# A causal convolution as full 128x128 matmuls, or as four 64x64 quarters of the array a tap

## The chip, the cores and the metric

The kernel runs on one core of a Trainium2 chip. Times are device microseconds of that core; the profile's times are microseconds from the start of its span unless they are marked ns. TensorE does the matmuls (PE in the profile, its weight loads PEld), VectorE (DVE) elementwise work and the scans, ScalarE (ACT) activations and most of the copies out of PSUM, GpSimd (POOL) further elementwise work and the indirect DMAs, SyncE (SP) issues the other DMAs.

## The reference, cut to what matters

```
xz = x @ in_proj_w.T + in_proj_b              # x: 4 batches x 2048 positions x 256
x_in, z = jnp.split(xz, 2, axis=-1)           # 512 channels each
x_pad = jnp.pad(x_in, ((0, 0), (3, 0), (0, 0)))
x_conv = sum(x_pad[:, k:k + L, :] * conv_w[None, None, :, k] for k in range(4)) + conv_b
x_conv = silu(x_conv)
x_dbl = x_conv @ x_proj_w.T                   # dt_low (64), B (16), C (16)
dt = softplus(dt_low @ dt_proj_w.T + dt_proj_b)
# scan over positions, 16 states for each of the 512 channels:
#   h = exp(dt * A) * h + (exp(dt * A) - 1) / A * B * x_conv
#   y = sum over the states of h * C, + D * x_conv
x = layernorm(x + (y * silu(z)) @ out_proj_w.T + out_proj_b)
# then 16 experts, the best 2 of each row, a shared expert and a second layernorm
```

Everything is float32. The change touches the line with the four taps.

## The kernel before

The first part of the program (`mamba`) works in 16 units of 512 positions. The 512 channels are four chunks of 128, one channel a partition. A unit has 64 items (4 chunks x 16 states): VectorE scans an item along the 512 positions, GpSimd or VectorE multiplies the result by C, and TensorE adds it into `y_ps` with a matmul by a diagonal (L1040). For the states of kind "f" TensorE also makes the scan's input with four small matmuls (L1062, `make_du`), for which VectorE's line L1226 waits.

The order of work is written out by hand. A unit is a loop over 64 slots, and in slot m each engine does item m and then whatever the tables place there. The table `PLACE` gives the slot in which each further tile of TensorE begins: `x0` to `x3` are the input projection, `c0` to `c3` the convolution, `low`, `bc`, `d0` to `d3` lead to dt, `T0` to `T3` are transposes, `r0` to `r3` the skip term, `z0` to `z3` the gate, `o0`, `o1` the output projection, `t0`, `t1`, `lg`, `pf` belong to the routing. A tile has one to four parts, and one part is done a slot. The tiles go in turn into two PSUM banks (`work`), so a tile can begin only when the tile two before it has been copied out; the semaphores are `filled` and `emptied`. The tiles of kind x, c, low, T, d for the next unit are made during this one.

A chunk's convolution is four matmuls of 128 rows by 128 columns by 512 positions, one for each tap (L1115): the weights are a diagonal matrix of the tap's factors (`dg_tap`), the moving data is `x_in`, shifted by one position a tap, with three columns of the previous unit in front. ScalarE copies the sum out with the bias (L856), in the slot after the tile's last part, and applies silu to two chunks at once in slots 10 and 38 (L957).

Every engine runs its instructions in the order in which they stand. An instruction that waits holds up all behind it on its engine.

Of the kernel before, what the change touches and what calls it, by code (L numbers as in the profile page):

```python
# [28 lines left out]
P = 128  # L29
T = 512  # L30
# [3 lines left out]
DI = 512  # L34
CH = DI // P
KT = DM // P
NS = 16
TAPS = 4
HALO = TAPS - 1
RANK = 64  # L40
TT = T // P
EPS = 1e-5
NE = 16
IF = 128
# [75 lines left out]
class Kept:  # L120

    def __init__(self, nc):
# [13 lines left out]
        self.full = sb("full", [P, P], BF16)  # L136
        self.rows = sb("x_tok", [P, TT, ROW])
        self.x_tok = self.rows[:, :, 0:DM]
        self.home_steps = sb("home_steps", [P, 2, TT])
        self.y_gated = sb("y_gated", [P, CH, T])  # L140
        self.room = sb("room", [P, (NE + 1) * DM])
        self.stats = sb("stats", [P, TT, 6])
        self.mean_var = sb("mean_var", [P, TT, 2])
        self.spread = sb("spread", [P, TT])
        self.shift = self.stats[:, :, 0]
# [24 lines left out]
def mamba(nc, d):  # L170
# [5 lines left out]
    with ExitStack() as ctx:  # L176
# [10 lines left out]
        w_in = sb("w_in", [P, KT, 2 * DI])  # L187
# [3 lines left out]
        b_in = sb("b_in", [P, 2 * CH])  # L191
        taps = sb("taps", [P, CH, TAPS])
# [9 lines left out]
        dg_tap = kept.room[:, 0:CH * TAPS * P].rearrange("p (c k t) -> p c k t", c=CH, k=TAPS)  # L202
# [19 lines left out]
        x_in = kept.room[:, CH * TAPS * P:CH * (TAPS * P + HALO + T)].rearrange("p (c t) -> p c t", c=CH)  # L222
# [24 lines left out]
        work = psum("work", [P, 2, T])  # L247
# [28 lines left out]
        filled = [sem(f"work_filled{q}") for q in range(2)]  # L276
# [62 lines left out]
        def pool_slot(s):  # L339
# [11 lines left out]
        NEXT = ["x0", "x1", "x2", "x3", "c0", "c1", "c2", "c3", "low", "bc", "d0", "d1", "T0", "T1", "z0", "z1"]  # L351
        OWN = ["d2", "d3", "T2", "T3", "r0", "r1", "r2", "r3", "z2", "z3"]
        ROUTING = ["o0", "o1", "t0", "t1", "lg", "pf"]
        PLACE = [("x1", 0), ("x0", 1), ("c0", 3), ("c1", 5), ("d3", 8), ("T2", 9), ("T3", 10), ("d2", 12), ("o0", 16), ("o1",
# [3 lines left out]
        U_AT = [-2, -1, None, 1, None, 6, 7, None, 8, None, 15, 18, 19, None, 25, None, 28, 31, None, 32, None, 37, 39, None, 41,  # L358
# [62 lines left out]
        def emptied_all(eng, plan, unit, tiles):  # L421

            most = {}
            for t in sorted(tiles, key=ORDER.get):
                most[plan.bank(t)] = t
            for bank, t in most.items():
                eng.wait_ge(emptied[bank], plan.before(t, unit) + 1)
# [588 lines left out]
        def _(pe):  # L1016
# [48 lines left out]
            def tile(u, plan, t, part):  # L1065

                n, q, nq = later(u), u[1] % 2, (u[1] + 1) % 2
                bank = plan.bank(t)
                if part == 0:
                    wait(pe, emptied[bank], plan.before(t, u))  # L1070
                out = work[:, bank]
                if t in ("t0", "t1"):
                    k = int(t[1])
                    pe.wait_ge(normed, count(u, TT, 0))
                    for tt in range(TT):
                        mm = nc.tensor.transpose(work[:, bank, tt * P:(tt + 1) * P], x_tok[:, tt, k * P:(k + 1) * P], ident[:])
                elif t == "lg":
                    logits = work[:, bank, 0:TT * NE].rearrange("p (t e) -> p t e", e=NE)
                    if part == 0:
                        emptied_all(pe, plan, u, ["t0", "t1"])  # L1080
                        nc.tensor.matmul(logits, ones[:], b_gate[:].unsqueeze(1).to_broadcast([1, TT, NE]), start=True, stop=False)
                    for k in range(KT):
                        mm = nc.tensor.matmul(logits[:, part], x1_t[:, k, part * P:(part + 1) * P], w_gate[:, k],
                                              start=False, stop=(part == TT - 1 and k == KT - 1))
                elif t == "pf":
                    pe.wait_ge(route, count(later(u, -1), ROUTE, 5))
                    mm = number_places(work[:, bank, 0:(TT + 1) * NE])
                elif t == "low":
                    c = part
                    if c % 2 == 0:  # L1090
                        pe.wait_ge(x_conv_ready, count(n, 2, c // 2 + 1))
                    mm = nc.tensor.matmul(work[0:RANK + 2 * NS, bank], w_x[:, c], x_conv[:, nq, c], start=(c == 0), stop=(c == CH - 1))
                elif t == "bc":
                    emptied_all(pe, plan, u, ["low"])
                    for k in range(TT):
                        mm = nc.tensor.matmul(work[:, bank, k * 2 * NS:(k + 1) * 2 * NS], bc_rows[:, k * P:(k + 1) * P],
                                              ident[RANK:RANK + 2 * NS, RANK:RANK + 2 * NS], start=True, stop=True)
                elif t[0] == "x":
                    if t in ("x0", "x1") and part == 0:
                        pe.wait_ge(x_t_in[nq], loads(n))  # L1100
                    m, k = int(t[1]), part
                    mm = nc.tensor.matmul(out, w_in[:, k, m * P:(m + 1) * P], x_t[:, nq, k], start=(k == 0), stop=(k == KT - 1))  # L1102
                elif t[0] == "z":
                    m, k = int(t[1]) + CH, part
                    src = q if t in ("z2", "z3") else nq
                    mm = nc.tensor.matmul(out, w_in[:, k, m * P:(m + 1) * P], x_t[:, src, k], start=(k == 0), stop=(k == KT - 1))  # L1106
                elif t[0] == "c":
                    c, k = int(t[1]), part
                    if plan is first and c < 2 and k == 0:
                        pe.wait_ge(diags_ready, 1)  # L1110
                        pe.wait_ge(later_in, 16 * (len(LATER) + 2))
                    if k == 0:
                        pe.wait_ge(halo_moved, count(n, 2, 1))
                        emptied_all(pe, plan, u, [f"x{c}"])
                    mm = nc.tensor.matmul(out, dg_tap[:, c, k], x_in[:, c, k:k + T], start=(k == 0), stop=(k == TAPS - 1))  # L1115
                elif t[0] == "T":
                    c = int(t[1])
                    own, src = (u, q) if c >= 2 else (n, nq)
                    pe.wait_ge(x_conv_ready, count(own, 2, c // 2 + 1))
                    for k in range(TT):  # L1120
                        mm = nc.tensor.transpose(work[:, bank, k * P:(k + 1) * P], x_conv[:, src, c, k * P:(k + 1) * P], ident[:])
                elif t[0] == "d":
                    c = int(t[1])
                    if c < 2:
                        emptied_all(pe, plan, u, ["low"])
                    mm = nc.tensor.matmul(out, w_dt[:, c * P:(c + 1) * P], dt_low, start=True, stop=True)
                elif t[0] == "r":
                    c = int(t[1])
                    if c == 0:
                        pe.wait_ge(both_ready, count(u, 1, 1))  # L1130
                    mm = nc.tensor.matmul(out, skip_rows[:, c * P:(c + 1) * P], both[:], start=True, stop=True)
                elif t[0] == "o":
                    if part == 0:
                        pe.wait_ge(gated, count(u, CH, 0))

                    tt, rest_of_it = divmod(part, 2)
                    tok = (2 * int(t[1]) + tt) * P
                    o = work[:, bank, tt * DM:(tt + 1) * DM]
                    if not rest_of_it:
                        nc.tensor.matmul(o, kept.full[0:2 * 32 + 1], b_out_parts[:], start=True, stop=False)  # L1140
                    for c in (range(1, CH) if rest_of_it else (0,)):
                        mm = nc.tensor.matmul(o, y_gated[:, c, tok:tok + P], w_out[:, c], start=False, stop=(c == CH - 1))
                if part == parts_of(t) - 1:
                    mm.then_inc(filled[bank], 1)
# [290 lines left out]
def moe_layout(g, chunks):  # L1435

    import numpy as np

    def stack(name):
        return np.concatenate([g[f"L0_ffn_experts_{name}"], g[f"L0_ffn_shared_{name}"][None]])  # L1440

    up = np.concatenate([stack("wg"), stack("wu")], axis=2)
    return {
        "w_gate": chunks(g["L0_ffn_gate_w"]),
        "b_gate": g["L0_ffn_gate_b"][None],
        "d_row": g["L0_attn_D"][None],
        "w_up": up.reshape(NE + 1, KT, P, 2 * IF).transpose(2, 0, 1, 3),
        "w_down": stack("wd").transpose(1, 0, 2),
    }
# [834 lines left out]
```

## Time and profile before

| what | value |
|---|---|
| time, median of 3 runs | 2742.09 us (2737.33 to 2742.41) |
| span of the profiled execution, first to last instruction | 2716.5 us |
| PE busy | 2518.4 us, 93% of the span |
| DVE busy | 2283.9 us, 84% |
| POOL busy | 2286.1 us, 84% |
| ACT busy | 1832.6 us, 67% |
| mean granted clock of TensorE | 0.975 |

The profile shows the profiled execution's span only; what lies around it is the difference to a run's time, 25.6 us with the median. PE's busy time includes the overlap of consecutive matmuls, so it says that there was always one in flight, not that the array was at its peak. One float32 matmul appears as two MATMUL records and two LDWEIGHTS records: 256 convolution matmuls are x512 in the profile.

### The profile page before, as it was taken

The page shows a single profiled execution, that of the slowest core. Times are in us where ns is not written, and L with a number is a line of the kernel's source. Part 1 is how long each engine was busy: PE and PEld are TensorE (multiplying, and loading weights), DVE is VectorE, ACT ScalarE, POOL GpSimd, SP SyncE. Part 2 cuts the span into 40 slices and gives each one's busy share as a digit, 9 for nine tenths or more (in the row PEclk, how much of TensorE's full clock was granted, in tenths as well). Part 3 has the DMA queues.
Part 4 walks back from the last instruction along what each step waited for, and adds up shares of the span by engine and source line. Part 5 has one row for each costly group of instructions (what it writes and reads, how often), then busy time and mean ns, then how long its engine had stood idle before and what let it go on. Part 6 is the DMA issues. An engine that isn't in the chain of part 4 may idle for free. (4 is left out here: it accounts for less than half of the span.)

```text
span 2716.5 us, 37230 instructions
## 1 busy us (share of the span) xinstructions
PE 2518.4 (93%) x9666; PEld 1447.6 (53%) x9666; DVE 2283.9 (84%) x3740; ACT 1832.6 (67%) x3655; POOL 2286.1 (84%) x2127
## 2 busy tenths in 40 slices
PE   6899999999999999999999999999999988799997
PEld 3445555555545455545555555455554544488874
DVE  3898989898989898889898998989898989755546
ACT  5576767777686767676868676777767675355537
POOL 2899898989898989899898989898989898666654
PEclk8999999999999999999999999999999989899999
DMA  3233343434333434343334334343333334478667
GB/s 89 96 112 113 107 129 103 130 101 125 111 118 108 119 106 121 113 120 115 113 119 116 111 111 127 105 130 101 125 110 117 112 106 138 156 218 249 206 202 245
DMA packets 249004, 349.65 MB, mean 129 GB/s; under 512 B 75863, under 2 KB 123611, under 8 KB 248412
## 3 DMA queue, kind: packets, MB, share of 16 engines
q1 hardware_dynamic: 233196, 302.47, 37.3%
q0 software_dynamic: 15600, 44.79, 4.7%
q8 instruction: 83, 1.36, 0.2%
q14 instruction: 125, 1.02, 0.1%
HBM read 288.72 MB, written 58.45 MB: 128 GB/s over the span
## 5 line engine op out<-in xcount | busy, mean ns | idle before, releaser
L685 POOL TENSOR_TENSOR hc<-h,c_rep 128x512 f32<-128x512 f32 x832 | 1048.2, 1271 | 99.8 <-DMA c_rep<-bc_rows 47.4
L1040 PE MATMUL y_ps<-hc,dg_inv 128*128 128x512 f32 x1664 | 857.6, 607 | 17.6 <-POOL hc L685 15.4
L668 POOL TENSOR_TENSOR h<-x_conv,b_rep 128x512 f32<-128x512 f32 x640 | 803.9, 1269 | 35.3 <-PE y_ps L1040 14.1
L1233 DVE TENSOR_TENSOR_SCAN h<-a_ps,carry,h 128x512 f32<-128x512 f32 x640 | 807.6, 1270 | 9.7 <-ACT score L836 5.4
L778 ACT ACTIVATE a_ps<-dt,a_mat 128x512 f32<-128x512 f32 x640 | 438.6, 687 | 411.4 <-DVE h L1233 408.0
L1062 PEld LDWEIGHTS g_ps<-b_steps,x_conv_rows 128*128 128x128 f32 x3072 | 404.2, 194 | 232.4 <-issue 200.4
L1217 DVE SCALAR_TENSOR_TENSOR h<-a_ps,h 128x512 f32<-128x512 f32 x640 | 428.3, 669 | 92.4 <-ACT a_ps L778 92.3
L1040 PEld LDWEIGHTS y_ps<-hc,dg_inv 128*128 128x128 f32 x1664 | 286.8, 191 | 305.2 <-issue 226.5
L1062 PE MATMUL g_ps<-b_steps,x_conv_rows 128*128 128x128 f32 x3072 | 413.5, 278 | 30.4 <-ACT x_conv_rows L861 16.9
L778 ACT ACTIVATE h<-dt,a_mat 128x512 f32<-128x512 f32 x384 | 268.9, 712 | 60.8 <-POOL hc L685 60.5
L1241 DVE TENSOR_TENSOR_SCAN h<-g_ps,carry,h 128x512 f32<-128x512 f32 x192 | 245.4, 1278 | 24.0 <-ACT h L778 20.6
L1115 PE MATMUL work<-room 128*128 128x512 f32 x512 | 248.8, 595 | 7.8 <-ACT room L849 7.8
L1040 PE MATMUL y_ps<-hc,ident 128*128 128x512 f32 x384 | 217.4, 651 | 38.7 <-DVE hc L1251 38.7
L1241 DVE TENSOR_TENSOR_SCAN g_ps<-g_ps,carry,h 128x512 f32<-128x512 f32 x192 | 246.9, 1286 | 6.3 <-DVE skip L1269 0.5
L1758 POOL DMA_INDIRECT y_planes<-gathered,home x144 | 138.6, 962 | 98.4 <-DVE gathered L2162 74.9
L1102 PE MATMUL work<-x_t,w_in 128*128 128x512 f32 x256 | 140.3, 645 | 63.1 <-DVE x_tok L1284 36.8
L1933 PE MATMUL banks<-w_up,gathered 128*128 x576 | 149.7, 383 | 0.0
L1106 PE MATMUL work<-x_t,w_in 128*128 128x512 f32 x256 | 142.3, 651 | 4.1 <-ACT dt L878 2.1
L1115 PEld LDWEIGHTS work<-room 128*128 128x128 f32 x512 | 91.6, 191 | 95.4 <-issue 94.2
L1251 DVE SCALAR_TENSOR_TENSOR hc<-g_ps,a_inv,c_rep 128x512 f32<-128x512 f32 x192 | 142.0, 739 | 0.0
L650 POOL DMA_INDIRECT slot_rows<-x_tok,place x120 | 121.6, 1013 | 23.2 <-issue 12.2
L1040 PEld LDWEIGHTS y_ps<-hc,ident 128*128 128x128 f32 x384 | 70.6, 200 | 117.8 <-issue 70.7
(269 smaller groups left out, 3479.6 us busy)
## 6 DMA issues: line engine op xcount, KB each, us to landing
c_rep<-bc_rows SPq DMA_DIRECT2D x512, 256.0 KB, 3.4
b_rep<-bc_rows SPq DMA_DIRECT2D x320, 256.0 KB, 3.7
gathered<-slot_rows SPq DMA_DIRECT2D x144, 129.5 KB, 3.5
gathered<-y_planes SPq DMA_DIRECT2D x32, 512.0 KB, 7.7
x_t<-in_x_t SPq DMA_DIRECT2D x16, 512.0 KB, 4.5
x_tok<-in_x_tok SPq DMA_DIRECT2D x16, 512.0 KB, 4.1
out<-x_t SPq DMA_DIRECT2D x16, 512.0 KB, 3.1
x_t_rows<-y_gated SPq DMA_DIRECT2D x15, 512.0 KB, 2.6
```

The lines of the kernel that those rows point to most:

```text
L668: nc.gpsimd.tensor_tensor(h[:, i % SLOTS, e], x_conv[:, u[1] % 2, chunk(i, e)], b_rep[:, n % BS], ALU.mult).then_inc(u_ready, 1)
L685: nc.gpsimd.tensor_tensor(hc[:, i % HCS, e], h[:, i % SLOTS, e], c_rep[:, i % CS], ALU.mult).then_inc(hc_pool, 1)
L778: nc.scalar.activation(out, dt[:, c], ACT.Exp, scale=a_mat[:, c, s:s + 1]).then_inc(made, 1)
L1040: nc.tensor.matmul(y_ps[:, e], by, hc[:, i % HCS, e], start=first_one, stop=(i % HALF == HALF - 1)).then_inc(summed, 1)
L1062: one = nc.tensor.matmul(g_ps[:, e, k * P:(k + 1) * P], x_rows[:, c, k], b_steps[:, f, k], start=True, stop=True)
L1106: mm = nc.tensor.matmul(out, w_in[:, k, m * P:(m + 1) * P], x_t[:, src, k], start=(k == 0), stop=(k == KT - 1))
L1115: mm = nc.tensor.matmul(out, dg_tap[:, c, k], x_in[:, c, k:k + T], start=(k == 0), stop=(k == TAPS - 1))
L1217: nc.vector.scalar_tensor_tensor(out=slot, in0=a_ps[:, e], scalar=1.0, in1=slot, op0=ALU.subtract, op1=ALU.mult).then_inc(b_ready, 1)
L1233: nc.vector.tensor_tensor_scan(slot, a_ps[:, e], slot, before_it, ALU.mult, ALU.add).then_inc(scanned, 1)
L1241: nc.vector.tensor_tensor_scan(out, g_ps[:, e], slot, before_it, ALU.add, ALU.mult).then_inc(scanned, 1)
L1251: nc.vector.scalar_tensor_tensor(out=hc[:, i % HCS, e], in0=g_ps[:, e], scalar=a_inv[:, c, s:s + 1], in1=c_rep[:, i % CS], op0=ALU.mult, o ...
L1933: one = nc.tensor.matmul(gu_ps[:, k % 2, 0:2 * IF], xt[:, k % 4, h * P:(h + 1) * P], w_up[:, e, h], start=(h == 0), stop=(h == KT - 1))
```

## The change

The two chunks of a pair (c0 with c1, c2 with c3) are convolved together. A diagonal 128x128 matrix has only zeros off its two diagonal 64x64 blocks; the change issues only such blocks. For each tap there are four matmuls of 64 rows by 64 columns by 512 positions, each in another quarter of the array. In the notation (input rows, output partitions) they are, as issued: chunk c rows 0-63 to 0-63; chunk c rows 64-127 to 64-127; chunk c+1 rows 0-63 to 64-127; chunk c+1 rows 64-127 to 0-63. The results of rows 0-63 go to the first tile's bank and those of rows 64-127 to the second's, so the channels of the input projection, its bias and the taps are laid out in another order on the host (`by_quarters`), and what comes out stands in the old order.

The tiles `c0` and `c2` keep their places in the sequence of banks, but do nothing themselves. Their work is done with `c1` and `c3`, a tap a slot, in slots 5 to 8 and 32 to 35. Before, `c0` ran in slots 3 to 6 and `c2` in 31 to 34.

```diff
-        PLACE = [("x1", 0), ("x0", 1), ("c0", 3), ("c1", 5), ("d3", 8), ...
-                 17), ("x2", 22), ("r0", 26), ("x3", 26), ("r1", 27), ("c2", 31), ("c3", 32), ("t1", 35), ...
+        PLACE = [("x1", 0), ("x0", 1), ("c0", 5), ("c1", 5), ("d3", 8), ...
+                 17), ("x2", 22), ("r0", 26), ("x3", 26), ("r1", 27), ("c2", 32), ("c3", 32), ("t1", 35), ...
...
-                elif t[0] == "c":
-                    c, k = int(t[1]), part
+                elif t in ("c0", "c2"):
+                    return
+                elif t in ("c1", "c3"):
+                    c, k = int(t[1]) - 1, part
...
                     if k == 0:
                         pe.wait_ge(halo_moved, count(n, 2, 1))
-                        emptied_all(pe, plan, u, [f"x{c}"])
-                    mm = nc.tensor.matmul(out, dg_tap[:, c, k], x_in[:, c, k:k + T], start=(k == 0), stop=(k == TAPS - 1))
+                        emptied_all(pe, plan, u, [f"x{c}", f"x{c + 1}"])
+                    banks = [work[:, plan.bank(f"c{c + e}")] for e in range(2)]
+                    for e in range(2):
+                        for half, rows in enumerate((slice(0, QUARTER), slice(QUARTER, P))):
+                            at = QUARTER * (e ^ half)
+                            mm = nc.tensor.matmul(banks[half][at:at + QUARTER], dg_tap[rows, c + e, k, rows], x_in[rows, c + e, k:k + T],
+                                                  start=(k == 0), stop=(k == TAPS - 1))
+                            if k == TAPS - 1 and e == 1 and half == 0:
+                                mm.then_inc(filled[plan.bank(f"c{c}")], 1)
...
+    def by_quarters(v):
+        v = v.reshape((CH // 2, 4, QUARTER) + v.shape[1:])
+        return v[:, [0, 3, 1, 2]].reshape((DI,) + v.shape[3:])
```

TensorE's program from slot 3 to slot 8 of a unit, before. The convolution is `work<-room`, in the four rows of one matmul and the two of two:

```order
L1115 MATMUL work<-room 128x512 [waits work_emptied1,halo_moved,work_emptied0]
L1040 MATMUL y_ps<-hc,dg_inv 128x512 [waits hc_pool,gated]
L1115 MATMUL work<-room 128x512
L1040 MATMUL y_ps<-hc,dg_inv 128x512 [waits hc_pool,gated]
L1062 MATMUL g_ps<-b_steps,x_conv_rows 128x128 [waits scanned,work_emptied1,b_steps_ready]
L1062 MATMUL g_ps<-b_steps,x_conv_rows 128x128 x3
L1115 MATMUL work<-room 128x512
L1115 MATMUL work<-room 128x512 [waits work_emptied0,halo_moved,work_emptied1]
L1040 MATMUL y_ps<-hc,dg_inv 128x512 [waits hc_pool]
```

The same place after the change, from the two `y_ps` matmuls of slots 4 and 5 to the tile d3 (`work<-low,dt_out`), which stands behind the last group:

```order
L1041 MATMUL y_ps<-hc,dg_inv 128x512 [waits hc_pool,gated] x2
L1063 MATMUL g_ps<-b_steps,x_conv_rows 128x128 [waits scanned,work_emptied1,b_steps_ready]
L1063 MATMUL g_ps<-b_steps,x_conv_rows 128x128 x3
L1122 MATMUL work<-room 64x512 [waits work_emptied0,halo_moved,work_emptied1]
L1122 MATMUL work<-room 64x512 x3
L1041 MATMUL y_ps<-hc,dg_inv 128x512 [waits hc_pool]
L1063 MATMUL g_ps<-b_steps,x_conv_rows 128x128 [waits scanned,work_emptied1,b_steps_ready]
L1063 MATMUL g_ps<-b_steps,x_conv_rows 128x128 x3
L1122 MATMUL work<-room 64x512 x4
L1041 MATMUL y_ps<-hc,dg_inv 128x512 [waits hc_pool]
L1122 MATMUL work<-room 64x512 x4
```

The two matmuls of slots 3 and 4 are gone, and in each of slots 5 to 8 a group of four stands between matmuls of the full array.

ScalarE's program in slots 7 to 9, before. `x_conv<-work` (L856) is the copy of c0, then of c1; `x_arg<-work` is the first copy of d3:

```order
L778 ACTIVATE a_ps<-dt,a_mat 128x512 [waits scanned]
L856 ACTIVATE x_conv<-work,b_conv 128x512 [waits skip_ready,u_ready,work_filled0]
L792 ACTIVATE carry<-h 128x2 [waits scanned]
L778 ACTIVATE a_ps<-dt,a_mat 128x512 [waits scanned]
L856 ACTIVATE x_conv<-work,b_conv 128x512 [waits work_filled1]
L877 ACTIVATE x_arg<-work,b_dt 128x512 [waits decay_ready,softplus_step,factor_ready,work_filled0]
```

And after:

```order
L779 ACTIVATE a_ps<-dt,a_mat 128x512 [waits scanned]
L793 ACTIVATE carry<-h 128x2 [waits scanned]
L779 ACTIVATE a_ps<-dt,a_mat 128x512 [waits scanned]
L857 ACTIVATE x_conv<-work,b_conv 128x512 [waits skip_ready,u_ready,work_filled0]
L857 ACTIVATE x_conv<-work,b_conv 128x512 [waits work_filled1]
L878 ACTIVATE x_arg<-work,b_dt 128x512 [waits decay_ready,softplus_step,factor_ready,work_filled0]
```

The copy of c0 moved behind one more `a_ps` activation, which waits for a scan.

## Rows read from the trace of the kernel before

**Rows 1.** The page: busy time of each engine.

```profile
PE 2518.4 (93%) x9666; PEld 1447.6 (53%) x9666; DVE 2283.9 (84%) x3740; ACT 1832.6 (67%) x3655; POOL 2286.1 (84%) x2127
```

**Rows 2.** Stretches of one unit: window, length, busy us of each engine (instructions), clock, DMA, GB/s.

```profile
1064.00:1091.00 27.00, 26.43 (x98) 13.87 (x97) 26.52 (x36) 15.62 (x29) 25.83 (x27) 1.00 0.31 89
1091.00:1114.00 23.00, 20.49 (x82) 12.54 (x80) 18.11 (x24) 16.11 (x25) 22.44 (x19) 0.99 0.61 176
1114.00:1133.00 19.00, 18.86 (x63) 9.89 (x64) 16.97 (x31) 11.85 (x22) 16.25 (x15) 0.92 0.23 72
1133.00:1150.00 17.00, 16.76 (x61) 8.71 (x60) 16.76 (x23) 10.88 (x24) 14.26 (x12) 1.00 0.29 103
1150.00:1185.00 35.00, 33.98 (x138) 18.50 (x136) 30.23 (x50) 27.30 (x57) 30.46 (x30) 1.00 0.43 110
1185.00:1207.30 22.30, 17.53 (x69) 9.60 (x69) 19.87 (x25) 20.50 (x41) 20.00 (x19) 1.00 0.38 128
sum 143.30, PE 134.05 PEld 73.10 DVE 128.45 ACT 102.25 POOL 129.25; mean PE 22.34 PEld 12.18 DVE 21.41 ACT 17.04 POOL 21.54
```

**Rows 3.** Waits in 1064 to 1207.2: who waited for whom, us, times, longest.

```profile
DVE g_ps L1226 <- PE g_ps L1062: 5.2, 6, 1.1
```

**Rows 4.** PE in order of time, slots 7 to 9: start, us, instructions, idle before.

```profile
1081.12 1.02 PE L1040 MATMUL y_ps<-hc,dg_inv 128*128 128x512 f32 x2
1081.97 1.02 PE L1115 MATMUL work<-room 128*128 128x512 f32 x2
1082.83 1.02 PE L1040 MATMUL y_ps<-hc,dg_inv 128*128 128x512 f32 x2
1083.69 1.02 PE L1115 MATMUL work<-room 128*128 128x512 f32 x2
1084.64 1.12 PE L1126 MATMUL work<-low,dt_out 64*128 64x512 f32 x2
```

**Rows 5.** PE in order of time, around a matmul of 7 rows.

```profile
1001.20 0.60 PE L1076 MATMUL work<-ident,x_tok 128*128 128x128 f32 x4
1001.64 1.02 PE L1040 MATMUL y_ps<-hc,dg_inv 128*128 128x512 f32 x2
1002.50 0.60 PE L1076 MATMUL work<-ident,x_tok 128*128 128x128 f32 x4
1003.03 1.12 PE L1131 MATMUL work<-both,skip_rows 7*128 7x512 f32 x2
1004.08 1.13 PE L1040 MATMUL y_ps<-hc,dg_inv 128*128 128x512 f32 x2
1005.04 1.05 PE L1062 MATMUL g_ps<-b_steps,x_conv_rows 128*128 128x128 f32 x8
```

**Rows 6.** PE in order of time, start of the program, a matmul of 6 columns.

```profile
19.46 0.59 PE L1115 MATMUL work<-room 128*128 128x512 f32 x1
19.98 1.04 PE L1168 MATMUL y_ps<-ident,a_inv 128*6 128x128 f32 x8
```

**Rows 7.** ACT in order of time, slots 7 to 9.

```profile
1080.46 0.69 ACT L856 ACTIVATE x_conv<-work,b_conv 128x512 f32<-128x512 f32 x1 [0.20 <-PE work L1115]
1084.75 0.69 ACT L778 ACTIVATE a_ps<-dt,a_mat 128x512 f32<-128x512 f32 x1 [3.51 <-DVE h L1233]
1085.38 0.67 ACT L856 ACTIVATE x_conv<-work,b_conv 128x512 f32<-128x512 f32 x1
1085.94 0.68 ACT L877 ACTIVATE x_arg<-work,b_dt 128x512 f32<-128x512 f32 x1
```

**Rows 8.** DVE in order of time, slot 14, behind the first pair.

```profile
1091.74 0.17 DVE L1226 TENSOR_TENSOR g_ps<-g_ps,minus_u 128x6 f32<-128x6 f32 x1 [0.62 <-PE g_ps L1062]
1093.29 1.28 DVE L1241 TENSOR_TENSOR_SCAN h<-g_ps,carry,h 128x512 f32<-128x512 f32 x1 [1.37 <-ACT h L778]
```

**Rows 9.** PE in order of time: its long idle times in the unit.

```profile
1114.14 2.07 PE L1102 MATMUL work<-x_t,w_in 128*128 128x512 f32 x2 [2.65 <-DVE x_tok L1284]
1185.89 1.13 PE L1040 MATMUL y_ps<-hc,ident 128*128 128x512 f32 x2 [1.92 <-DVE hc L1251]
```

More of the change, by code:

```diff
@@ L41 @@
 TT = T // P
+QUARTER = P // 2
 EPS = 1e-5
@@ L353, in mamba @@
         ROUTING = ["o0", "o1", "t0", "t1", "lg", "pf"]
-        PLACE = [("x1", 0), ("x0", 1), ("c0", 3), ("c1", 5), ("d3", 8), ("T2", 9), ("T3", 10), ("d2", 12), ("o0", 16), ("o1",
[1 row of a table removed]
+        PLACE = [("x1", 0), ("x0", 1), ("c0", 5), ("c1", 5), ("d3", 8), ("T2", 9), ("T3", 10), ("d2", 12), ("o0", 16), ("o1",
[1 row of a table added]
                  ("low", 37), ("r3", 38), ("bc", 41), ("lg", 44), ("d1", 48), ("d0", 48), ("z1", 49), ("z3", 50), ("pf", 54),
@@ L1440, in stack @@
         return np.concatenate([g[f"L0_ffn_experts_{name}"], g[f"L0_ffn_shared_{name}"][None]])
+    def by_quarters(v):
+        v = v.reshape((CH // 2, 4, QUARTER) + v.shape[1:])
+        return v[:, [0, 3, 1, 2]].reshape((DI,) + v.shape[3:])
+    in_proj, in_bias = g["L0_attn_in_proj_w"], g["L0_attn_in_proj_b"]
     up = np.concatenate([stack("wg"), stack("wu")], axis=2)
     return {
+        "w_in": chunks(np.concatenate([by_quarters(in_proj[:DI]), in_proj[DI:]]).T),
+        "b_in": chunks(np.concatenate([by_quarters(in_bias[:DI]), in_bias[DI:]])),
+        "taps": chunks(by_quarters(g["L0_attn_conv_w"])),
         "w_gate": chunks(g["L0_ffn_gate_w"]),
```

2 rows, old and new, of the table PLACE are left out of this document.

## The prediction

> **What bounds the kernel now.** I read the busy shares first: PE is busy 93% of the span, VectorE and GpSimd 84% each [rows 1]. So TensorE is the fullest engine, but the other two are near, and a share over the whole span doesn't say which one sets the pace. I then cut one unit of the scan part (1064 to 1207.3, a period of 143.3 us) into stretches [rows 2]. PE is busy 134.05 of 143.30 us, and idle 9.25. The first pair of chunks is convolved in the first stretch and the second pair in the fourth. There VectorE is as full as TensorE: 26.52 and 26.43 of 27.00 us, 16.76 and 16.76 of 17.00. So at both places two engines bind at once. Work taken from PE there gains little, because VectorE has no room; work added to PE delays at once what VectorE waits for. That it does wait for PE shows in the list of waits: 5.2 us a unit, six times [rows 3]. After the second pair PE stays full for a long stretch (33.98 of 35.00), so a delay from there isn't taken back before 1185. The third thing to read is PE's long idle times, which are the room for added work: 2.65 us at 1114 and 1.92 us at 1186, both behind VectorE [rows 9], the rest in pieces under 1.5 us.
>
> **What a convolution matmul costs.** One 128x512 float32 matmul is two records. In a run without idle a matmul begins 0.86 us after the one before (1081.12, 1081.97, 1082.83, 1083.69) [rows 4], so each of its two passes takes 0.43 us of the array. A record's 1.02 us for x2 is longer only because the end of a pass overlaps the next. A pair of chunks is 8 matmuls, 6.9 us; a unit has two pairs, 13.7 us; 16 units (the first one at the start of the program) make 220 us.
>
> **The change, part 1: the mode of the array.** Each group of four quarters stands alone between matmuls of the full array. What it costs to go to a part of the array and back can be read at the skip term, 7 rows by 128 columns [rows 5]. The four transposes before it take 0.53 us where they take 0.44 before a full matmul (1001.20 to 1001.64), the matmul itself holds 1.05 us to the next start where 0.86 is normal, and the full matmul behind it 0.96 instead of 0.86: together 0.39 us for one excursion. At the program's start a matmul of 128x6 begins 0.52 us after a pass that takes 0.43 [rows 6], so limiting the columns costs the same 0.09 on the way in. Eight groups a unit: 8 x 0.39 = 3.1 us.
>
> **Part 2: four quarters at once, or in a row.** No two matmuls of the trace use different parts of the array back to back, so the overlap isn't shown and I bound it. Streaming 512 positions takes 0.43 us a pass for 7 rows too (1.05 less 0.19 for two), so a quarter's pass isn't shorter. If all four quarters ran at once, a group would be 2 x 0.43 = 0.86; if none did, 8 x 0.43 = 3.44. Before, the same work (two matmuls) was 1.72.
> What decides is the order of the passes. The program is issued in order, and the two passes of one matmul stand side by side: pass 1 of quarter A, pass 2 of A, pass 1 of B, and so on. Pass 2 of A needs the same quarter as pass 1 of A, so it starts 0.43 later; B's pass 1 may start with it; B's pass 2 must wait for its own pass 1, and C starts with that. With starts that never pass each other, as in [rows 4, 5], only neighbours of different quarters overlap: four quarters take 5 passes, 2.15 us. This is the value I take; the bounds are 0.86 and 3.44. A group is then 2.15 + 0.39 = 2.54 us against 1.72: +0.82, or +6.6 us a unit of PE's time.
> The Trainium skill weighs on both sides here (TensorE: Matmul & The Clock Gate, Part 3: Packing small matmuls). It says that matmuls on different tiles of the array run concurrently, a pack lasting about one matmul plus 4 ns a tile; by that a group would be the 0.86 of the lower bound. The same section says that matmuls keep program order in start and in end, which with two passes a matmul gives the 5 passes. No run here shows either yet.
>
> **Part 3: the moved places.** Slots 3 and 4 lose one matmul each, 1.72 us a unit; that is already in the 8 counted, but they were filler in slots where PE otherwise waits for the products `hc`, so part of it comes back as idle. The copy of c0 moves on ScalarE from slot 7 to slot 9, behind an `a_ps` activation that waits 3.51 us for a scan until 1084.75 [rows 7]. Before, c0's bank was free by 1081.15 and PE began d3 at 1084.64 without a wait [rows 4]. Now d3 can't begin before 1084.75 + 0.63 + 0.6 = 1086.0, even if PE is there earlier. Queued behind d3 on PE are the `y_ps` matmul of slot 9 (for which GpSimd's next products wait), T2, and the matmuls L1062 for slot 14. With groups of 2.54 us PE gets to d3 at 1084.64 + 3.3 = 1087.9, so this wait is hidden except for the copy of c0 itself, about 0.3 us (0.67 from the third quarter's end, less the 0.43 that the fourth still takes). At slot 35 the tile t1 needs c2's bank in the same way: again about 0.3.
> Nothing else costs: the DMAs, the host's order of channels (the same bytes) and the number of copies and silus stay. The 32 weight loads of a pair where there were 16 are hidden as now, since each lies beside the pass of another quarter; were that cover gone, rows 5 price each uncovered one at about 0.10 us.
>
> **The sum.** A unit: +6.6 for the groups and +0.6 for the two bank waits = +7.2 us on PE. In the first pair the matmuls for slot 14 come 3.6 us late; VectorE already waited 0.62 there for PE and then 1.37 for ScalarE [rows 8], and ScalarE itself is held by the copies of c0, c1 and d3, so 2.5 to 3.6 reach VectorE. What can absorb is PE's idle 9.25, but most of it is behind VectorE, which is late as well. I let about a quarter be absorbed: +5.3 us a unit. The last unit makes no convolution for a next one, and in the first sixteenth, at the start of the program, groups follow each other without full matmuls between, so that it costs nothing: 15 x 5.3 = +80. On the span: 2716.5 + 80 = 2796; the 25.6 us to the median of the runs shown stay, so 2742 + 80 = **2822 us**. If nothing is absorbed it is 2742 + 108 = 2850, if half is, 2796.
>
> **The rivals.** A, all four at once: a group is 0.86 + 0.39 = 1.25, -0.47, and PE has 3.8 us a unit less. For it: the quarters touch different rows, columns and banks. But PE then stands before d3 from about 1082.8 until 1086.0, 1.4 later than before, in a stretch where VectorE is full; the gain must come between the pairs. Net -1.5 to +1 us a unit, likeliest -0.5: 2735, and 2720 at best. This is the side on which the kernel gets faster; it decides from a group under about 1.5 us.
> B, only two quarters at a time: if the two that share rows can't stream together but passes may be reordered, a group is 4 passes, 1.72 + 0.39: +3.1 us a unit, two thirds reaching the end, 15 x 2.1 = 32: 2774.
> C, no overlap at all, so the change does not do what it says: 3.44 + 0.39 = 3.83, +2.11 a group, +16.9 a unit, less some 2.5 absorbed: 15 x 14.4 = 216: 2958. Against it speaks only that nothing in the order requires it.
>
> **How the numbers follow.** Chances: the forecast 0.52, A 0.24, B 0.10, C 0.14. Faster or slower than 0.2% (5.5 us) is what a measurement of this kernel can tell. A is faster in most of its range (0.18), unchanged in 0.04, slower in 0.02; the rest is slower. I leave a further 0.01 to faster: 0.19, 0.05, 0.76. The forecast's own range is 2790 to 2855; the one given reaches down through B and nearly all of A and leaves C out: 2715 to 2880.
>
> **What would show it.** In the profile after: the starts of the eight records of a group. Steps of 0.43 between pairs that start together, and 2.1 to 2.2 us from the first start to the last end of streaming, confirm the forecast; four starts within 0.1 us mean A; eight steps of 0.43 mean C. The full matmul behind a group should begin 0.09 late. The steady period should be 148 to 149 us instead of 143.3, and VectorE's wait for L1062 (now L1063) should grow from 5.2 us a unit to 8 or more. The forecast falls if a group takes 1.3 us or less, or if the period stays at 143 with groups of 2.5 us, which would mean that PE's idle time absorbs it all.

## The result and the profile after

| what | before | after |
|---|---|---|
| time, median (runs) | 2739.71 us (4) | 2774.22 us (4), 2773.14 to 2775.81 |
| ratio, 95% interval | | 1.0131 (1.0116 to 1.0145) |
| span of the profiled execution | 2716.5 us | 2771.7 us |
| ratio on a second chip, same kernels | | 1.0153 (1.0136 to 1.0169) |

The change makes the kernel 1.3 to 1.5% slower. The sign was forecast; the size was not (80 us forecast, 34.5 measured), and neither was the reason, as the rows show.

The page of after, busy time of each engine. It answers to [rows 1]:

```profile
PE 2484.7 (90%) x10178; PEld 1391.6 (50%) x10178; DVE 2288.2 (83%) x3740; ACT 1835.5 (66%) x3655; POOL 2290.5 (83%) x2127
```

PE is busy 34 us less, and the program is longer. The convolution alone, by line (busy us, mean ns, then PE's idle time before it): 147.2 us where L1115 was busy 248.8.

```profile
L1122 PE MATMUL work<-room 64*64 64x512 f32 x1024 | 147.2, 651 | 1.7 <-ACT room L850 1.7
```

So the quarters overlap. How far, one group shows. These are the records of L1122 that begin between 1088.2 and 1088.3 us of after (operation, count, durations in ns, first and last start):

```profile
L1122 PEld LDWEIGHTS work<-room x5: 129/129/133, 1088.2 to 1088.3; 64*64 64x64 f32 x5
L1122 PE MATMUL work<-room x4: 640/640/640, 1088.2 to 1088.3; 64*64 64x512 f32 x4
```

All four quarters begin their first pass together (in the records' own nanoseconds the starts are 1088.242, .249, .255 and .262), and the four second passes begin at 1088.72 to 1088.74. The group among its neighbours, PE of after in order of time, answers to [rows 4]:

```profile
1088.24 1.09 PE L1122 MATMUL work<-room 64*64 64x512 f32 x8
1089.26 1.12 PE L1041 MATMUL y_ps<-hc,dg_inv 128*128 128x512 f32 x2
1090.22 1.05 PE L1063 MATMUL g_ps<-b_steps,x_conv_rows 128*128 128x128 f32 x8
```

From the group to the next matmul it is 1.02 us, and that matmul holds 0.96 instead of 0.86. With the 0.09 before the group, a group costs 1.21 us where the same work cost 1.72.

Then where does the time go? For each of the 13 units 2 to 14 (counted from 0) I took the starts of VectorE's 64 scans (one a slot) and split the unit's period at slots 8, 14, 32 and 44. Means in us, worked out from one trace of each kernel; e1 and so on are the experiments below. They ran on two other chips: e5, e7, e8 and e9 on one, the rest on the other.

```
kernel                      slots 0-8  8-14   14-32  32-44  44-64  unit
before                        16.83   13.41   41.77  26.74  44.66  143.4
before, another chip          16.84   13.42   41.76  26.75  44.68  143.4
after                         17.61   15.41   41.82  27.27  44.66  146.8
after, another chip (e7)      17.10   15.12   42.33  27.27  44.60  146.4
e1 places only                17.22   15.00   42.80  27.64  44.69  147.4
e2 copies first               16.70   13.91   43.41  27.27  44.64  145.9
e3 filler                     16.60   14.95   42.46  27.27  44.67  146.0
e4 both pairs a slot earlier  16.60   13.03   42.68  26.35  44.12  142.8
e5 first pair earlier         16.60   13.03   41.81  27.27  44.65  143.4
e8 full matmuls, e4's slots   16.83   13.28   42.42  26.35  44.46  143.3
e9 two taps a slot            17.19   13.03   42.68  26.35  44.12  143.4
e10 two taps, e4's slots      17.19   13.09   42.75  26.35  44.08  143.5
```

After loses 0.8 us before slot 8, 2.0 between 8 and 14, and 0.53 behind the second pair; the rest of a unit is as it was. All of it lies at the two places to which the work was moved.

**Slots 3 to 8: idle time and the clock.** PE of after in order of time:

```profile
792.57 1.12 PE L1041 MATMUL y_ps<-hc,dg_inv 128*128 128x512 f32 x2 [1.45 <-DVE y_gated L1273]
794.05 1.80 PE L1063 MATMUL g_ps<-b_steps,x_conv_rows 128*128 128x128 f32 x8 [0.36 <-DVE h L1251]
795.78 1.99 PE L1122 MATMUL work<-room 64*64 64x512 f32 x8
797.70 1.13 PE L1041 MATMUL y_ps<-hc,dg_inv 128*128 128x512 f32 x2
```

Slots 3 and 4 have nothing left to do between their `y_ps` matmuls, so PE waits 1.45 us for VectorE. Then the eight records of L1063 take 1.80 us where they take 1.05 elsewhere, and the group takes 1.99 instead of 1.09. The stretches 790 to 794 and 794 to 798 of the same unit say why (the seventh number group is the granted clock, then the DMA share and GB/s):

```profile
790.00:794.00 4.00, 2.24 (x4) 0.58 (x4) 3.86 (x6) 2.04 (x4) 3.81 (x4) 1.00 0.49 164
794.00:798.00 4.00, 3.95 (x17) 2.14 (x18) 4.00 (x5) 0.51 (x1) 3.81 (x4) 0.57 0.32 103
```

Over most of the second stretch TensorE had 1.2 GHz instead of 2.4. Between 200 and 2200 us the records of after hold 32 such falls with 109 us at the low clock; those of before 16 with 55 us. What it costs VectorE, in order of time: it waits 1.20 us in slot 8. Such a fall comes in 10 of the 13 units.

```profile
799.82 0.17 DVE L1236 TENSOR_TENSOR g_ps<-g_ps,minus_u 128x6 f32<-128x6 f32 x1 [1.20 <-PE g_ps L1063]
```

**Slots 8 to 14: the copy behind the scan.** ScalarE of after, answering to [rows 7], PE, answering to [rows 4], and VectorE, all in the same unit:

```profile
804.90 0.69 ACT L779 ACTIVATE a_ps<-dt,a_mat 128x512 f32<-128x512 f32 x1 [5.42 <-DVE h L1243]
805.53 1.25 ACT L857 ACTIVATE x_conv<-work,b_conv 128x512 f32<-128x512 f32 x2
```

```profile
803.80 1.09 PE L1122 MATMUL work<-room 64*64 64x512 f32 x8
806.25 1.12 PE L1136 MATMUL work<-low,dt_out 64*128 64x512 f32 x2 [1.37 <-ACT x_conv L857]
807.31 1.45 PE L1041 MATMUL y_ps<-hc,dg_inv 128*128 128x512 f32 x2
```

```profile
808.87 0.22 DVE L1259 TENSOR_SCALAR carry<-g_ps,minus_u 128x1 f32<-128x1 f32 x1 [1.45 <-PE y_ps L1041]
814.60 0.17 DVE L1236 TENSOR_TENSOR g_ps<-g_ps,minus_u 128x6 f32<-128x6 f32 x1 [1.77 <-PE g_ps L1063]
```

The last group was done by 804.8, but ScalarE sat behind an `a_ps` activation until 805.5, so d3 began at 806.25. Behind it on PE stood the `y_ps` matmul for which VectorE waited at 808.87. That idle time too is followed by a fall of the clock (the matmul at 807.31 takes 1.45 us for 1.02). In slot 14 VectorE waits 1.77 us for L1063 [rows 8: 0.62].

How much of this is the copy and how much the clock, three traces of this loop say together (after, e7 and e6, which differs only at the program's start; 39 units). In 23 units the clock falls in both places, in 12 in neither:

```
                           slots 0-8  8-14   14-32  32-44  44-64  unit
no fall before slot 14       16.60   14.73   42.79  27.27  44.61  146.0
a fall in both places        17.92   15.48   41.46  27.27  44.65  146.8
```

Without any fall before slot 14 the unit still takes 2.6 us more than before. The two falls add 2.1 us up to slot 14, but 1.3 of these come back by slot 32: the clock falls at slot 22 or 23 in 10 of the 12 units and in none of the 23. So the falls before slot 14 are worth 0.8 us a unit.

**Behind the second pair.** The waits of after in 350 to 2150 us (us, times, longest):

```profile
DVE g_ps L1236 <- PE g_ps L1063: 82.0, 82, 2.0
DVE carry L1259 <- PE y_ps L1041: 19.6, 13, 2.4
PE y_ps L1041 <- DVE y_gated L1273: 18.9, 13, 1.5
PE work L1136 <- ACT x_conv L857: 18.6, 13, 1.6
PE work L1077 <- ACT x_conv L857: 9.5, 12, 0.8
```

Of the five the first stood before at 59.6 us over the same stretch, 74 times. The others are new in the list. The last is t1 (L1077), 0.8 us a unit.

### The profile page after: what moved, and what is told of

The parts are those of the page before. It is cut to its first block and busy times, and to the rows that moved or that the text cites. A ratio compares the mean times of both kernels' runs of the same rounds, so it can differ in the third digit from the quotient of the medians.

```text
span 2771.7 us, 38253 instructions
## 1 busy us (share of the span) xinstructions
PE 2484.7 (90%) x10178; PEld 1391.6 (50%) x10178; DVE 2288.2 (83%) x3740; ACT 1835.5 (66%) x3655; POOL 2290.5 (83%) x2127
## 3 DMA queue, kind: packets, MB, share of 16 engines
q14 instruction: 125, 1.02, 0.1%
## 5 line engine op out<-in xcount | busy, mean ns | idle before, releaser
L1041 PE MATMUL y_ps<-hc,dg_inv 128*128 128x512 f32 x1664 | 878.6, 620 | 49.6 <-POOL hc L686 28.1
L1063 PEld LDWEIGHTS g_ps<-b_steps,x_conv_rows 128*128 128x128 f32 x3072 | 413.0, 198 | 256.8 <-issue 222.7
L1063 PE MATMUL g_ps<-b_steps,x_conv_rows 128*128 128x128 f32 x3072 | 423.4, 282 | 44.4 <-ACT x_conv_rows L862 19.7
L779 ACT ACTIVATE h<-dt,a_mat 128x512 f32<-128x512 f32 x384 | 268.6, 711 | 59.6 <-POOL hc L686 59.3
L1103 PE MATMUL work<-x_t,w_in 128*128 128x512 f32 x256 | 138.4, 638 | 58.8 <-DVE x_tok L1294 31.0
L1122 PE MATMUL work<-room 64*64 64x512 f32 x1024 | 147.2, 651 | 1.7 <-ACT room L850 1.7
L1107 PE MATMUL work<-x_t,w_in 128*128 128x512 f32 x256 | 136.8, 629 | 4.6 <-ACT dt L879 2.1
L2164 DVE TENSOR_TENSOR gathered<-gathered,banks 128x128 f32<-128x128 f32 x144 | 41.4, 287 | 117.4 <-ACT gathered L1831 77.2
L713 POOL TENSOR_TENSOR dt<-dt,poly 128x512 f32<-128x512 f32 x64 | 81.3, 1271 | 68.4 <-DVE poly L1345 68.4
```

The lines of the kernel that those rows point to most:

```text
L779: nc.scalar.activation(out, dt[:, c], ACT.Exp, scale=a_mat[:, c, s:s + 1]).then_inc(made, 1)
L1041: nc.tensor.matmul(y_ps[:, e], by, hc[:, i % HCS, e], start=first_one, stop=(i % HALF == HALF - 1)).then_inc(summed, 1)
L1063: one = nc.tensor.matmul(g_ps[:, e, k * P:(k + 1) * P], x_rows[:, c, k], b_steps[:, f, k], start=True, stop=True)
L1122: mm = nc.tensor.matmul(banks[half][at:at + QUARTER], dg_tap[rows, c + e, k, rows], x_in[rows, c + e, k:k + T], start=(k == 0), stop=(k == ...
```

## The experiments

Each ratio is to the kernel before on the same chip, with its 95% interval. The theories: **P**, the moved places cost (a late copy, an idle PE and its clock); **S**, going in and out of the quarter mode costs.

**e7, the changed kernel again**, beside other experiments.

> The changed kernel as it is, on the same chip as the three kernels beside it. All theories: a ratio of 1.012 to 1.015 to the kernel before.

Measured 2760.47 us, 1.0153 (1.0136 to 1.0169). Its trace is of the fastest of its four runs, 2755.25 us.

**e1, the places without the quarters.** Edit of the kernel before:

```diff
-("c0", 3), ("c1", 5) ... ("c2", 31), ("c3", 32)
+("c0", 5), ("c1", 5) ... ("c2", 32), ("c3", 32)
```

> The kernel before with the change's places only (c0, c1 in slots 5 to 8, c2, c3 in 32 to 35), still full 128x128 matmuls. Theory P (what costs is the place: the copies of c0 and c1 stand behind a scan-bound activation on ScalarE, and the emptied slots 3 and 4 leave PE idle and its clock falls): slower than before by 3 to 5 us a unit, since PE also has the 3.8 us of unsaved work, so 2785 to 2815 us. Theory S (what costs is going in and out of the quarter mode, eight times a unit): the places alone cost nothing, 2740 to 2750 us.

Measured 2768.52 us, 1.0172 (1.0155 to 1.0189), where before had 2722.26: +46 us; as a ratio this is in P's range, 1.016 to 1.027 of 2740. The places alone cost at least what the whole change costs; a unit takes 147.4 us. So S isn't needed for the loss. Eight full matmuls in four slots also crowd TensorE, a rival to the late copy; e8 below, as crowded one slot earlier, answers it.

**e2, the copy ahead of the scan-bound activation.** Edit of the changed kernel, on ScalarE only:

```diff
+                    for t in plan.whole_at(m - 1):
+                        if t[0] == "c":
+                            tile(u, plan, t)
                     a_s_at(u, plan, m)
```

(and `weave` leaves these tiles out).

> The changed kernel, with ScalarE's copies of a convolved pair ahead of the a_ps activation of the same slot instead of behind it. Theory P: d3's wait for the copy (1.4 to 1.6 us before) falls to about 0.8, VectorE's wait for y_ps in slot 12 goes, and the kernel gains about 1 us a unit against the changed one (2774): 2755 to 2765 us. Theory S: the wait was not what sets the time, 2770 to 2780 us.

Measured 2745.08 us, 1.0084 (1.0068 to 1.0101): 0.7% faster than e7. Slots 8 to 14 fall from 15.12 to 13.91 us, and PE's wait for the copy to 0.79 us, as expected; VectorE's wait for `y_ps` falls to 0.3 us a unit and doesn't go. Most of the gain is lost again in slots 14 to 32 (43.41 against 42.33), so in the traces a unit gains 0.5 us, half of what I expected.

**e3, a filler in the emptied slots.** Edit of the changed kernel: in slots 3 and 4 TensorE also runs

```diff
+                emptied_all(pe, plan, u, ["x0", "x1"])
+                wait(pe, emptied[bank], plan.before("c0", u))
+                nc.tensor.matmul(work[:, bank], dg_tap[:, 0, 0], x_in[:, 0, 0:T], start=True, stop=True)
```

> The changed kernel with one more full 128x512 matmul (0.86 us, its result is overwritten) in each of the slots 3 and 4 of a unit, in the place of the convolution that was moved away. Theory P with the clock: TensorE is no longer idle there, its clock stays at 2.4 GHz in slots 5 and 6, and the 1.1 us that the scan of slot 8 lost in 11 of 13 units comes back: about 2760 us although PE has 1.7 us a unit more to do. Rival (only the amount of PE's work counts): 15 x 1.7 = 26 us slower than the changed kernel, about 2800 us.

Measured 2755.09 us, 1.0123 (1.0106 to 1.0140): not slower by 26 us, but a little faster than e7 (the intervals of the two ratios just overlap). PE of e3 in the place of the rows at 792.57 above:

```profile
794.36 1.02 PE L1163 MATMUL work<-room 128*128 128x512 f32 x2
795.41 1.13 PE L1041 MATMUL y_ps<-hc,dg_inv 128*128 128x512 f32 x2
796.89 1.13 PE L1063 MATMUL g_ps<-b_steps,x_conv_rows 128*128 128x128 f32 x8 [0.36 <-DVE h L1262]
797.95 1.09 PE L1122 MATMUL work<-room 64*64 64x512 f32 x8
```

L1063 takes 1.13 us and the group 1.09 again. The long step between the scans 7 and 8 (2.7 us for 1.4) stood in 5 of 13 units of e7 and in none of e3. 1.7 us a unit of useless work made the kernel no slower. The clock's part is smaller than the late copy's: 0.5 us a unit here, 0.8 to 1.0 up to slot 8 in the first trace, where more units had it.

That the filler kept the clock up is only in part shown. All these kernels but e3 have the same idle times there, 1.45 and 0.36 us, and the fall follows in 10 of 13 units of after, 8 of e6, 5 of e7, 3 of e1 and 1 of e2 (and in none of e9, where 11 units have them). So the idle time doesn't bring the fall by itself; what else decides stays open.

**e4, both pairs a slot earlier; e5, the first pair only.** Edits of the changed kernel:

```diff
-("c0", 5), ("c1", 5) ... ("c2", 32), ("c3", 32)
+("c0", 4), ("c1", 4) ... ("c2", 31), ("c3", 31)    # e4; e5 has the first two alone
```

> The changed kernel with its groups one slot earlier: slots 4 to 7 and 31 to 34. Theory P: ScalarE copies c0 and c1 in slot 8, ahead of the scan-bound activation, d3 starts without a wait, PE's idle time in slots 3 and 4 is shorter; the kernel is about as fast as the one before, 2730 to 2750 us. Theory S: the excursions are as many, 2765 to 2780 us.

> The changed kernel with only the first pair a slot earlier (slots 4 to 7); the second stays in 32 to 35. Theory P1 (nearly all of the loss is in the first pair, where the scan of slot 14 came 3.1 us late of 3.5): ratio 0.995 to 1.000 to before. Rival P2 (the second pair's place, where t1 waits for the copy of c2, costs about half): ratio 1.003 to 1.008.

Measured e4 2700.60 us, 0.9924 (0.9908 to 0.9941), the fastest kernel, faster than either theory allowed; e5 2710.72 us, 0.9966 (0.9953 to 0.9978), as P1 expected. ScalarE of e4 in order of time:

```profile
1068.06 1.27 ACT L857 ACTIVATE x_conv<-work,b_conv 128x512 f32<-128x512 f32 x2 [1.82 <-PE work L1122]
1070.37 0.69 ACT L779 ACTIVATE a_ps<-dt,a_mat 128x512 f32<-128x512 f32 x1 [1.04 <-DVE h L1243]
```

Now ScalarE is there before PE, and the copies stand ahead of the activation that waits. Slots 8 to 14 take 13.03 us, less than before the change, and the clock falls in none of the 13 units before slot 14. In e5 the second pair keeps its wait (L1077 10.3 us in 13 units, slots 32 to 44 27.27); in e4 that wait is gone and they take 26.35.

**e8, full matmuls in e4's slots**, to price the quarters themselves. Edit of the kernel before: the places of e4.

> The kernel before, with full 128x128 matmuls, in the places of the fastest kernel so far (slots 4 to 7 and 31 to 34; that one had a ratio of 0.992). It says what the quarters are worth where no copy is late. Theory Q (the 3.8 us of PE's work that the quarters save a unit are worth something once the copies are in place): 1.000 to 1.008, slower than the kernel with quarters. Rival (VectorE binds there and the quarters save nothing; the places alone made the 0.992): 0.990 to 0.995.

Measured 2713.73 us, 0.9983 (0.9974 to 0.9993). It lies between the two ranges: I had expected this kernel to be no faster than before. The places give 0.2%, the quarters in them another 0.6%. With e1 and e4 it makes a square: a slot later costs 4.0 us a unit with full matmuls (e8 to e1) and 3.6 to 4.0 with quarters (e4 to e7 and after), so the loss is the place, whatever the matmuls. PE's own saving is 8 x 0.51 = 4.1 us a unit; the period falls by 0.56 (143.34 to 142.78). The start of the program gains 5.0 us once (first scan at 57.7 us, e8 62.7).

**e9 and e10, two taps a slot**: half as many excursions, in slots 5, 6 and 32, 33 (e9), or 4, 5 and 31, 32 (e10).

```diff
-        PARTS = {"x": 2, "z": 2, "o": 4, "c": TAPS, "low": 4, "lg": TT}
+        PARTS = {"x": 2, "z": 2, "o": 4, "c": TAPS // 2, "low": 4, "lg": TT}
...
+                    for k in (2 * part, 2 * part + 1):
```

> The changed kernel with two taps a slot: a pair is two groups of eight quarters in slots 5, 6 and 32, 33, so half as many excursions from the full array (4 a unit in place of 8, 1.6 us less for PE), and the copies come two slots earlier. Theory P: the copies of c0 and c1 stand ahead of the scan-bound activation, so the loss of slots 12 and 14 is gone; the idle time in slots 3 and 4 and its lower clock stay: ratio 0.992 to 1.000. Theory S (excursions cost): the gain against the changed kernel is no more than 1.6 us a unit, ratio 1.004 or above.

> Two taps a slot and a slot earlier: groups of eight quarters in slots 4, 5 and 31, 32. Theory P (idle time of PE and the place of the copies cost, excursions cost only where PE binds): all three gains together, ratio 0.988 to 0.993, at least as fast as the kernel with one tap a slot from slot 4 (0.9924). Rival (a pair done early leaves PE idle in slots 6 to 8, and its clock falls there): 0.994 to 1.000.

Measured e9 2710.07 us, 0.9968 (0.9957 to 0.9980), e10 2708.90 us, 0.9962 (0.9949 to 0.9976). e9 is 1.8% faster than e7: its copies come in slot 7. e10 misses what I expected: it is slower than e4, though it has fewer excursions. Its time is in the rival's range, but the rival's clock doesn't fall in slots 3 to 8 in any of the 13 units. Both take 17.19 us up to slot 8, 0.6 more than e4. The group of eight stands before the L1063 matmuls for which VectorE waits in slot 8; that this is the cause I read from the order and didn't test.

**e6, another order of the quarters**, at the program's start only, for c2 and c3: all taps of a quarter, then the next quarter.

> The changed kernel with another order of the 16 quarter matmuls of c2 and c3 at the program's start only: all four taps of one quarter, then the next quarter's, where the changed kernel issues the four quarters of a tap together and takes 3.5 us for them (start 24.3 us). Theory O (matmuls start in program order; the two passes of one matmul do not hold up the matmul behind it, but a matmul whose quarter is busy does): 13 times 0.86, 11.2 us. Rival (each quarter of the array has a queue of its own): 3.5 us as before.

The line in e6 (23 to 33 us), and in e7 with the four quarters of a tap together (24 to 28.5 us):

```profile
L1126 PE MATMUL work<-room 64*64 64x512 f32 x32 | 8.9, 594 | 0.9 <-ACT room L850 0.9
```

```profile
L1122 PE MATMUL work<-room 64*64 64x512 f32 x32 | 3.7, 594 | 0.9 <-ACT room L850 0.9
```

8.9 us is neither theory's number (the whole program took 2761.20 us, one run). The starts say what happens: quarter A's taps begin at 23.61, 24.49, 25.35 and 26.21; quarter B's first at 25.36, with A's third; C's at 27.13, with B's third. So one matmul can wait for its busy quarter without stopping those behind it, and the next one for that quarter stops them: 3 x 1.77 + 3.44 = 8.8 us.

**The kernel before again**, for a trace on the chip of e1 to e4.

> The kernel before, for a trace from the same chip as the experiments. The scans of a unit should stand as in the first trace of it, except where the clock of TensorE falls: in slot 26 the experiments of this chip are 1.2 us late and this one is expected to be too.

Measured 2717.03 us. The scans stand as in the first trace in every segment of the table, and slot 26 is not late in its typical unit. So that expectation was wrong: the 0.6 to 1.6 us that the experiments but e5 and e6 lose in slots 14 to 32 are theirs. They go with the fall of TensorE's clock after its wait at slot 22 (at 1114 in [rows 9]): in these slots it falls in 2 or 3 of 13 units of before, before again, after, e5 and e6, and in 7 to 11 of e1, e2, e3, e4, e7, e8, e9 and e10. VectorE's wait for the skip matmul was 2.5 us in 3 units before, and 10.6 us in 10 units of e4. Why it strikes in more units there stays open.

## Why the prediction was wrong

**Part 1, the mode of the array: right.** Forecast 0.39 us an excursion; measured 0.35 (0.09 before the group, 1.02 + 0.96 after it less 2 x 0.86).

**Part 2, four quarters in a row: this step failed.** "Four quarters take 5 passes, 2.15 us": they take 2, 0.93 us from the first start to the end of the second passes, and a group costs 1.21 instead of 2.54. I took each pass for an entry of its own in the order of issue. The trace shows that the order holds between matmuls and not between their passes, and e6 that even a matmul for a busy quarter can wait aside. The Trainium skill (TensorE: Matmul & The Clock Gate, Part 3) has a pack of tiles last about one matmul and 4 ns a tile; the trace agrees nearly, with 7 ns between the four starts and 0.93 us for the pack where one matmul is 0.86. The same section has matmuls start and end in program order, from which I had the 5 passes. The group agrees with it, once a float32 matmul is taken as one matmul and not as two; e6 doesn't, since quarter B's first matmul starts at 25.36 and quarter A's fourth, issued before it, at 26.21. The term was +0.82 us a group and should have been -0.51: over the eight groups of a unit -4.1 us of PE's time for the forecast +6.6.

**Part 3, the moved places: mechanism right, far too small.** I saw that the copy of c0 goes behind an activation waiting for a scan and that d3 then waits, 1.4 us in rival A; measured 1.4 to 1.6. But I took that wait for PE's alone. Through the `y_ps` matmul behind it, and where the clock falls too, it reached VectorE with 2.0 us a unit in slots 8 to 14 (1.3 of them in units without a fall; e2 gives 1.2 back, e5 all). And I wrote of the emptied slots that part "comes back as idle" and gave that no price: in 10 of 13 units the clock then falls just where VectorE needs L1063, 0.8 us a unit up to slot 8. For t1 I had 0.3; it was 0.8 on PE and 0.53 for the unit.

**The sum and rival A.** Right was A's group (1.25 forecast, 1.21 measured), and wrong its range of -1.5 to +1 us a unit; it came to +3.4. The forecast of 5.3 was nearer in number than A's likeliest -0.5, by two errors of opposite sign: the groups too dear, the places too cheap. Rival B's number, 2774, is the measured one to the microsecond, and that is luck: its groups would have taken 2.11 us, and they took 1.21. 13 units x 3.4 us = 44, and the scans of the whole program, first to last, did take 43.0 us longer (2281.7 to 2324.7); the start gave 4.0 back. Rivals B and C fall with the starts of the records. (In the chances, slower adds up to 0.77 and unchanged to 0.04 where 0.76 and 0.05 stand; nothing hangs on it.)

**The 25.6 us around the span** were no such thing. In every later run the time is 1.8 to 2.1 us above its span. The profiled execution of before was simply faster than the timed ones. The part behind the last scan, which the change doesn't touch, takes 387.4 us in the first trace of after and 369.7 to 371.1 in all others, the first of before too; why, no trace here says. So the spans of the two first traces don't compare. Those of e7 and of the kernel before again do: e7's is 38.2 us longer, 42.6 between the first scan and the last, less 4.5 at the start.

**What would show it.** I had named the right rows: four starts within 0.1 us mean A, and they do. Also there: VectorE's wait for L1063 up from 59.6 to 82.0 us in 350 to 2150, 5 to about 6.6 us a unit, where I had asked for 8.

## What to carry to other kernels

Work saved on the busiest engine is worth little where another is as full: 4.1 us a unit of TensorE's time gave 0.56. What a move does to the neighbours counts for more, so read where the instruction that frees a buffer lands in its own engine's order: behind an instruction that waits for the critical engine it cost more than the saving here, and one slot earlier it cost nothing. And before emptying a slot, ask what keeps TensorE busy there: the clock fell behind such a place in many units, though not in all.

## What the hardware showed

- Four 64x64 float32 matmuls in different quarters of the array run at the same time, with both their passes: 0.93 us for 512 positions, 1.21 with the way in and out, against 0.86 for one full matmul.
- One matmul that waits for its busy quarter lets those behind it start, a second one for the same quarter doesn't (8.9 us for 16 matmuls in that order, 3.7 with the quarters in turn).
- Idle times of 1.45 and 0.36 us of TensorE in an otherwise full stretch were followed by the 1.2 GHz level in 23 of 39 units of the changed loop (three traces), and in 1 to 3 of 13 of two kernels with the same idle times (e2, e1). A useless matmul in each of slots 3 and 4, 1.7 us a unit, cost nothing in all.
